# Three of eight final clips move from VectorE to GpSimd, in a new order of the memory stage

## The reference

```python
def entmax15(x):
    x = (x - jnp.max(x, -1, keepdims=True)) / 2.0
    ...
    return jnp.square(jnp.clip(x - tau_star, 0.0, None))
...
for _ in range(NUM_STEPS):                                  # 3
    scores = jnp.einsum('bhsd,hnd->bhsn', xi, K) * beta     # 8 heads, 256 slots
    w = entmax15(scores)
    xi = jnp.einsum('bhsn,hnd->bhsd', w, V)
out = xi.transpose(0, 2, 1, 3).reshape(B, S, H * hd) @ Wo.T
```

## Time and profile before

| | us |
|---|---|
| median of 3 runs | 1848.6 (1843.72 to 1849.27) |
| the profiled execution | 1844.72 |
| its span | 1842.9 |
| first to last `bound` of the memory stage (48 of them, 47 slots) | 516.92 to 1294.44 |
| last `out_norm` of the stage ends | 1348.39 |

### The profile page before, as it was taken

The page is one execution under the profiler, slowest core; times in us unless marked ns, Lnnn a source line. Parts: engine busy times, 40 slices in busy tenths (PEclk is TensorE's granted clock), DMA queues, the critical chain, the costliest instruction groups (busy, mean ns, idle before and its releaser), DMA issues. The chain is left out here.

```text
span 1842.9 us, 25960 instructions
## 1 busy us (share of the span) xinstructions
PE 1595.7 (87%) x7554; PEld 1120.9 (61%) x7554; DVE 1375.4 (75%) x3613; ACT 1181.6 (64%) x2865; POOL 601.2 (33%) x1908
## 2 busy tenths in 40 slices
PE   5799999989748889978898879888879899999987
PEld 2546656565646667866786668766645556555554
DVE  6666757562359999999999999999744565776646
ACT  3244343412159999999999999999637665665630
POOL 3504233240134455545554455544310100101000
PEclk9799999999888889999998889988989999999989
DMA  5000000000300000000000000000000000000000
GB/s 227 1 1 1 1 1 1 1 1 0 109 1 1 1 1 1 1 1 1 1 1 1 1 1 1 1 1 1 1 0 1 1 1 1 1 13 1 12 1 23
DMA packets 6717, 19.23 MB, mean 10 GB/s; under 512 B 1072, under 2 KB 4144, under 8 KB 5296
## 3 DMA queue, kind: packets, MB, share of 16 engines
q1 hardware_dynamic: 6576, 17.58, 2.6%
HBM read 15.48 MB, written 2.10 MB: 10 GB/s over the span
## 5 line engine op out<-in xcount | busy, mean ns | idle before, releaser
L1610 ACT ACTIVATE mem_arena<-mem_arena,r_shift 128x256 f32<-128x256 f32 x864 | 385.2, 511 | 23.0 <-POOL r_shift L1529 23.0
L1340 DVE BATCH_NORM_STATS2 r_moments<-mem_arena 128x6 f32<-128x512 f32 x576 | 379.9, 690 | 9.4 <-ACT mem_arena L1610 6.3
L1689 PE MATMUL r_bank<-arena,r_wT 128*128 128x256 f32 x1024 | 232.3, 386 | 4.2 <-ACT mem_arena L1610 3.7
L1689 PEld LDWEIGHTS r_bank<-arena,r_wT 128*128 128x128 f32 x1024 | 195.1, 194 | 35.3 <-issue 9.0
L1705 PE MATMUL r_bank<-ident,mem_arena 128*128 128x128 f32 x576 | 109.6, 322 | 71.8 <-DVE mem_arena L1356 71.7
L1317 DVE MAX8 r_top<-r_bank 128x8 f32<-128x256 f32 x384 | 145.3, 405 | 17.1 <-PE r_bank L1689 16.9
L1699 PE MATMUL r_bank<-arena,ident 128*128 128x256 f32 x384 | 142.4, 458 | 12.6 <-ACT r_wT L1636 12.4
L2243 ACT ACTIVATE arena<-arena,e_NM 128x512 f32<-128x512 f32 (+3 forms) x256 | 134.3, 558 | 29.5 <-DVE e_NM L1931 29.5
L1705 PEld LDWEIGHTS r_bank<-ident,mem_arena 128*128 128x128 f32 x576 | 79.8, 164 | 114.1 <-DVE mem_arena L1356 104.6
L1689 PE MATMUL r_bank<-arena,r_xnT 128*128 128x256 f32 x512 | 120.8, 396 | 24.1 <-ACT mem_arena L1610 23.7
L1610 ACT ACTIVATE r_u<-r_u,r_shift 128x256 f32<-128x256 f32 x288 | 131.8, 510 | 5.6 <-POOL r_shift L1529 5.6
(11 more groups left out here) (328 smaller groups left out, 3222.1 us busy)
## 6 DMA issues: line engine op xcount, KB each, us to landing
w<-in_w SPq DMA_DIRECT2D x3, 1024.0 KB, 14.4
out_x<-X SPq DMA_DIRECT2D x4, 512.0 KB, 2.9
X<-in_x SPq DMA_DIRECT2D x1, 1536.0 KB, 10.6
w_in<-in_w_in SPq DMA_DIRECT2D x1, 1156.0 KB, 6.4
mem_arena<-in_wq SPq DMA_DIRECT2D x1, 1024.0 KB, 17.5
mem_arena<-in_wo SPq DMA_DIRECT2D x1, 1024.0 KB, 21.0
gate<-in_gate SPq DMA_DIRECT2D x1, 1024.0 KB, 7.8
up<-in_up SPq DMA_DIRECT2D x1, 1024.0 KB, 9.8
```

The costliest lines, as they stand in the source:

```text
L1340: last = dve.bn_stats(moments[:, a.lane, 2 * p:2 * p + 2, :].rearrange("p two c -> p (two c)"), u[a.lane][:, 2 * p:2 * p + 2, :].rearrange ...
L1610: last = act.activation(u[a.lane][:, h, :], u[a.lane][:, h, :] if k else scores[:, h, :], ACT.Relu, bias=shift[:, a.lane, h:h + 1])
L1689: last = pe.matmul(scores[:, h, :], lhs, (G1 if a.first else G2)[:, h, i, :], start=i == 0, stop=i == 1)
```

## The change

The final clips of heads 5, 6 and 7 are made by POOL, those of heads 0 to 4 by DVE. The PE waits before a transpose name the semaphore of the engine that made the heads of that pair. The lists of all four engine loops are replaced. `DVE_CLIPS` and DVE's `clip` allow clips of the other passes on DVE; the tuple is empty for all passes, so they issue nothing. ACT's unused `weights` is removed. The first slot is one earlier and the last one earlier.

```diff
-DVE_HEADS = (0, 1, 2, 3, 4, 5, 6, 7)
-ACT_HEADS = ()
-FIRST_SLOT, LAST_SLOT = -3, TILES * STEPS - 1 + 9
+DVE_HEADS = (0, 1, 2, 3, 4)
+POOL_HEADS = (5, 6, 7)
+DVE_CLIPS = ((), (), (), ())
+FIRST_SLOT, LAST_SLOT = -4, TILES * STEPS - 1 + 8
...
+            def weights(a, *heads):
+                if not a.live:
+                    return
+                pool.wait_ge(shift_ready[PASSES - 1], of_unit(a))
+                for h in heads:
+                    pool.tensor_scalar(u[a.lane][:, h, :], u[a.lane][:, h, :], shift[:, a.lane, h:h + 1], 0.0, ALU.add,
+                                       ALU.max).then_inc(pool_weights, 1)
...
-                running_sum(Unit(n - 4), 0)
-                running_sum(Unit(n - 4), 1)
+                newton(Unit(n - 1), 2)
+                running_sum(Unit(n + 1), 1)
+                running_sum(Unit(n + 1), 2)
...
-                    pe.wait_ge(dve_weights, of_unit(a, len(DVE_HEADS), sum(h <= 2 * p + 1 for h in DVE_HEADS)))
-                    if any(h // 2 == p for h in ACT_HEADS):
-                        pe.wait_ge(act_weights, of_unit(a, len(ACT_HEADS), sum(h <= 2 * p + 1 for h in ACT_HEADS)))
+                    if any(h // 2 == p for h in DVE_HEADS):
+                        pe.wait_ge(dve_weights, of_unit(a, len(DVE_HEADS), sum(h <= 2 * p + 1 for h in DVE_HEADS)))
+                    if any(h // 2 == p for h in POOL_HEADS):
+                        pe.wait_ge(pool_weights, of_unit(a, len(POOL_HEADS), sum(h <= 2 * p + 1 for h in POOL_HEADS)))
```

More of the change, by code:

```diff
@@ L1333, in bound, with clip @@
                 dve.tensor_reduce(neg8[:, a.lane], back[:, a.lane], AX.X, ALU.max, negate=True).then_inc(bound_ready, 1)
+            def clip(a, k, *heads):
+                if not a.live:
+                    return
+                dve.wait_ge(shift_ready[k - 1], of_unit(a))
+                for h in heads:
+                    last = dve.tensor_scalar(u[a.lane][:, h, :], u[a.lane][:, h, :], shift[:, a.lane, h:h + 1], 0.0,
+                                             ALU.add, ALU.max)
+                    if h % 2:
+                        last.then_inc(dve_clipped[k], 1)
             def take_moments(a, k, *pairs):
@@ L1417, in _ @@
[L1417 to L1426, removed]
+                largest(Unit(n - 4), 0, 1)
@@ L1428, in _ @@
+                out_stats(Unit(n - 8))
+                bound(Unit(n - 4))
+                tile_stats(Unit(n + 1))
+                take_moments(Unit(n - 6), 3, 3)
+                invert(Unit(n - 6), 3)
+                out_norm(Unit(n - 8))
+                take_moments(Unit(n - 4), 0, 0, 1, 2)
+                take_moments(Unit(n - 5), 2, 0)
         @block.gpsimd
@@ L1557, in _ @@
             for n in range(FIRST_SLOT, LAST_SLOT + 1):
-                if n == LAST_SLOT - 2:
+                if n == LAST_SLOT - 7:
                     first_batch_norms()
[L1560 to L1578, removed]
-                running_sum(Unit(n - 4), 0)
-                running_sum(Unit(n - 4), 1)
+                newton(Unit(n - 1), 2)
+                running_sum(Unit(n + 1), 1)
+                running_sum(Unit(n + 1), 2)
+                mean_and_gap(Unit(n + 1))
+                mean_square(Unit(n + 1))
+                add_gap(Unit(n + 1))
+                add_room(Unit(n + 1))
+                second_moment(Unit(n - 0), 1)
+                step_back(Unit(n + 1))
+                newton(Unit(n - 0), 1)
+                start(Unit(n + 1))
+                out_rstd(Unit(n - 3))
+                second_moment(Unit(n - 1), 3)
+                tile_rstd(Unit(n + 4))
+                newton(Unit(n - 1), 3)
+                weights(Unit(n - 1), 5, 6)
+                second_moment(Unit(n + 1), 0)
+                newton(Unit(n + 1), 0)
+                weights(Unit(n - 1), 7)
+                second_moment(Unit(n - 0), 2)
+                centre(Unit(n + 2))
+                square(Unit(n + 2))
+                running_sum(Unit(n + 2), 0)
         @block.scalar
@@ L1619, in newton_root @@
                 act.activation(root[:, a.lane], s2[:, a.lane], ACT.Sqrt, scale=1.0 / NMEM).then_inc(root_ready[k], 1)
[L1621 to L1627, removed]
             def columns(a, *pairs):
@@ L1723, in _ @@
             for n in range(FIRST_SLOT, LAST_SLOT + 1):
[L1724 to L1732, removed]
+                transpose(Unit(n - 4), 3)
+                score(Unit(n - 0), 0, 1, 2, 3)
+                output(Unit(n - 4), 0, 1, 2)
+                tile_transpose(Unit(n + 2))
+                transpose(Unit(n - 3), 0)
+                output(Unit(n - 4), 3)
+                transpose(Unit(n - 3), 1, 2)
 def experts_block(nc, T, out):
```

108 lines of the change are left out of this document (57 added, 51 removed).

## The result

| | before | after |
|---|---|---|
| median us (range, runs) | 1847.0 (1843.7 to 1849.3, 4) | 1873.0 (1871.7 to 1876.5, 4) |
| profiled execution / its span | 1844.7 / 1842.9 | 1872.1 / 1870.3 |
| granted clock, whole span | 0.937 | 0.919 |
| first to last `bound` | 777.5 | 800.65 |
| last `bound` to the last row added | 53.9 | 55.5 |

The changed kernel is slower: ratio 1.0134 [1.0112, 1.0156], where 0.9957 was forecast. The time lies outside the range of 1822 to 1856.

A forecast was written before the change was run, and what follows sets the result against it. DVE was taken to bound plain slots and PE output slots, with a loop across engines setting plain slots after the change. Steady part -4 and end -4 gave -8 us, 1841 on the median's scale, range 1822 to 1856.

The forecast's parts named there:

- the steady part: First to last bound: 35 slots at 16.02, 12 output slots at 17.4, plus 4, 773.5 against 777.5: -4 us.
- rival 2: Scores in the deciding loop: PE's lower clock makes the kernel slower, +19 us if 10 slots see it, 1860; chance 0.15.
- The loop at full clock: Chain across engines, once per slot, from A's pass 0 clips to the next: 16.02 us, against 15.9 for a plain slot.
- The clock of PE: Scores at 1.2 GHz throughout cost 1.94 us more per slot; the forecast left 4 us for the first few slots only.
- Slots with a first step: Slots taking in rows of a new tile: the same 16.0 us instead of 16.3 to 16.8.
- DVE's list: DVE's work in a slot falls to about 14.5 or 14.6 us, so DVE waits and no longer bounds it.
- Output slots: The 12 slots holding an output, bounded by PE: 17.4 us each, against 17.3 before.
- The end: Last unit's first clip to last row added, 52.8 us before: a chain of outputs, shorter by 4 us.
- turns of transposes: At the end, one turn instead of two between an output's matmuls, about 0.87 each; over three outputs 2.6 us less.
- POOL's clips: Three final clips on POOL per slot, 0.64 us each (0.31 to 1.05), fit its room and cost nothing.
- Rival 1: DVE stays the bound, plain slots near 15.2: -32 us, 1817, half-way cases about 1828; chance 0.20 with these.
- Rival 4: Shared port: POOL's clips lock out DVE instructions, 31 us without room on DVE; 1856 if half came through; chance 0.03.

The follow-up runs named there:

- the first edit: All eight final clips on DVE, none on POOL, in the changed kernel with the rest of its new order kept: 1872.1 us, ratio 1.0135 to the kernel before.

## Why the prediction was wrong

The step that failed is the steady part at 35 x 16.02: it put the cost of PE's lower clock at nothing, and rival 2, which held it, was given 0.15 on the argument that gaps like these leave a plain slot at 0.93. The runs show 18 slots at 0.80 in the new order, 17 to 18 us that filler matmuls bring back. That is two thirds of the 27.4; the rest is in the terms below.

- **The loop at full clock: right.** 16.06 to 16.08 against 16.02, each term within 0.1. That it and not DVE's list is the bound is shown by the first edit: DVE gets 0.6 back and the slot stays.
- **The clock of PE: left out of the sum.** The rival spoke of 10 slots at 1.94. There were 18, each 1.02 over 16.02: 18.4 us. The price per slot was too high, since only the last transposes and the first scores run slow; the fourth window of the earlier trace rows had shown it, 16.80 against 15.90. The number of slots was too low. The argument against the rival (gaps of 2.3, 1.4 and 0.9, as in slots of before at 0.93) was the error. Measured gaps are 2.21 and 0.91. What the 0.93 of before meant is shown below the list. In the old order the clock costs 6 us, in the new 18 (both filler runs, medians).
- **Slots with a first step: off.** 16.0 was forecast instead of up to 16.8. Some of them are among the eighteen; with the clock held those are 16.1 to 16.3. The one ahead of the first output slot is 16.5 to 16.7 with and without filler, and the slot behind the last output slot 16.6 to 16.8. These six lie 4.1 us over 16.02, which the clock does not explain; why was not looked into.
- **DVE's list: 14.6 forecast, 15.10 measured.** Three clips are 0.6 of busy time (15.70 to 15.10). It changes nothing in the sum, since DVE is not the bound.
- **Output slots: off by 0.35 each.** 17.4 forecast, 17.74 measured on average, 4.1 us over 12. ACT waits up to 1.0 for the transposes of a pair behind output matmuls, then its pass 0 is late, and PE starts the scores 0.97 behind it, as in plain slots. This is read from the rows; the edit meant to remove the wait brought 1.6 us in all, so it is not shown to be the whole.
- **The end: wrong sign.** -4 forecast, +1.6 measured. `first_batch_norms` makes 3.6 of that (shown); the walk had left out this group of instructions, which issues in one slot only. Most of the remaining 2 fits the turns of transposes: of the three of 0.87 that were to go, one shows. With the norms moved the last four tiles' rows are added 12.2, 11.0 and 10.0 us after each other, before the change 11.8, 11.8 and 10.0.
- **POOL's clips: price wrong, verdict right.** 0.64 taken, range 0.31 to 1.05, measured 1.14. The two clips take 2.26 where 2.0 of room was counted, and `second_moment` behind them starts at T + 5.32, against T + 4.97 without clips on POOL: 0.35 late, and the slot is no longer for it (shown by the first edit). Where the room is gone it costs: 8 us with a fourth clip; one clip in the old order cost 26 us with what it did to the clock.
- **Rival 1** (DVE stays bound): no slot is near 15.2. **Rival 4** (the port): DVE's final clips take 0.33 to 0.35 in the slot of 1011.32, but none of them runs beside a clip of POOL there; of all 240 six do, at the end of the stage, and take 0.34 to 0.56. DVE's moments and maxima that run beside POOL's clips are as long as the others (0.69 and 0.41), so 31 us of locking are not there.

PE of the kernel before, in and behind the first plain slot of the earlier trace rows (0.93):

```profile
797.80 0.66 PE L1705 MATMUL r_bank<-ident,mem_arena 128*128 128x128 f32 x4 [1.98 <-DVE mem_arena L1356]
799.07 1.17 PE L1699 MATMUL r_bank<-arena,ident 128*128 128x256 f32 x2 [0.62 <-ACT r_wT L1636]
...
802.59 7.07 PE L1689 MATMUL r_bank<-arena,r_wT 128*128 128x256 f32 x32
```

The clock falls there too (two fillers take 1.17), but only behind the last gap, 3.5 us ahead of the scores, and is back when they start: 7.07. In the new order it falls behind the second gap, 4.7 us ahead of the scores, and they take 7.72. So the 0.93 did not show that such gaps are harmless, only that the low level ended in time.

The sum again: -8 was forecast. Slots at low clock +18.4, the six beside the output slots +4.1, output slots +4.1, eight slots at 16.08 +0.5, end +5.6, make +32.7, so +24.7 (the first three slots were costed right at 4). The span grew 27.4; the rest is the 2.8 of the fourth block less the 0.2 by which the stage begins earlier. That block's code is unchanged. From the last row added to the end of the span the profiled executions of all runs take 493.8 to 499.1 us (494.7 with no clips on POOL, 497.4 in the kernel after), so the 2.8 are no effect of the change that could be told from noise.

## What to carry to other kernels

Taking work from the busiest engine pays only if the order's chain across engines, once round per slot, is shorter than that engine's list: walk it term by term before counting the relief. Where PE stands in that chain, count its gaps as well: a new order with the same busy times can lose more to a lower clock than it wins, and matmuls that fill the gaps tell the two apart in one run. An instruction that stands in one slot only (norms of the next stage) is part of the walk of that slot.

## What was not expected of the hardware

A POOL tensor_scalar (add, max; one f32 input of 128x256) took 1.14 us here, in 144 instructions, against 0.34 on DVE and 0.40 per clip on ACT.

```profile
L1550 POOL TENSOR_SCALAR mem_arena<-mem_arena,r_shift 128x256 f32<-128x256 f32 x108 | 122.3, 1140 | 3.5
```

It is dearer than a two-input instruction on twice the elements (1.047 for 512). The Trainium skill, GPSIMD Engine Reference, section 3.1 on elementwise work, gives about 1.8 cycles an element as the best case, of a tight unrolled loop, and about 2.6 for two inputs. At the 1.2 GHz of that page 1.14 us is 5.3 cycles an element, by this estimate, and the measurement decides.

PE fell to 1.2 GHz in the middle of a slot behind two waits of 2.21 and 0.91 us, and the lower level reached into the scores. With the first gap filled but for 0.49 it was granted 1.00 in every slot from the fifth on, with PE busy 14.57 us of 16.07 instead of 12.22 of 16.06. In the old order gaps of 1.98 and 0.62 brought the lower level too, but it ended ahead of the scores.
